# A two-layer graph kernel on one Trainium2 core: a third staging buffer for transposed halves, and their order by row tiles

## The chip, the cores and the metric

The kernel runs on 1 core of one Trainium2 chip. The metric is device time in microseconds, as the median of several runs. A profile is one execution with the hardware profiler; its times are used for single instructions.

## The reference

x is 2048 x 512, adj is 2048 x 2048, both fp32. The constants scale and quantise; what is computed is

```python
h = maximum(layernorm(x), 0)
# layer 0: quantised inputs (15 levels) times quantised weights (7 levels)
support = relu(matmul(quant(h), quant_w(weight)) * scales)
x = x + matmul(adj / s, quant(support)) * s * delta
# layer 1: y = C2 @ Dinv (adj_sym + I) Dinv @ h2, with C2 = adj, adj_sym = (adj + adj.T) / 2
h = maximum(layernorm(x), 0)
deg = sum(adj_sym + eye, axis=1)
x = x + (adj @ (deg**-.5 * (adj_sym + eye) * deg**-.5)) @ h
```

## The kernel before

Both products with adj need it transposed on the partitions. The tile `at` holds adj transposed for all 16 row tiles of 128 rows, each entry as two fp16 halves: hi is the rounded value (times 256) and lo is the rest. adj comes in by 32 units; unit u is one half (1024 columns) of row tile u // 2, 128 x 1024 fp32, 512 KB. There are two ways from a unit to `at`:

- A unit is turned: TensorE transposes it by eight 128 x 128 fp32 transposes into PSUM (`turn`, L1041), ScalarE writes the hi half (`hi_turned`, L487), VectorE adds up the columns (`column_sum`, L702) and writes the lo half (`lo_turned`, L715). ScalarE adds up the rows (`row_sum`, L467).
- A unit is moved: ScalarE writes the hi half untransposed to a stage (`hi_rows`, L476, with the row sums), VectorE the lo half (`lo_rows`, L720), and SyncE issues a DMA transpose for each half from the stage to `at` (`move`, L323). There are two stages, used in turn, in the space of row tile 14 of `at`; a stage is free again when both transposes of the unit that used it have landed (`wait_moved`). Unit 29 has a place of its own in tile 15. Moved are the odd units 3 to 29, and 14, 18, 22 (`EVEN`). For an even moved unit VectorE adds up the columns from `at` (`column_sum_late`, L708). GpSimd adds the odd units 1 to 29 to one tile `acc` (L441, L444), which is turned once, as "acc", and reduced by L848.

Until they are needed for `at`, the places of later row tiles hold loads (`in_tile`), so that a transposed unit of tile 6 or later may be written only when the units waiting in its tile are used up (`waited_in`, `free_slot`).

The stage that the change touches is layer 0. Product r is the 32 matmuls of row tile r (`layer0`, L1062), from r = 0 to 15 in order. Product r waits for its two transposed units, and from 2 to 13 also for `x1_ready` of tile r - 2, whose PSUM bank it uses again. For r = 1 to 13 every engine has a list: `TURNS[r]` and `MOVES[r]` give the units. TensorE turns the first unit of `TURNS[r]` ahead of product r and others inside it. ScalarE and VectorE go through the same r in the order of their programs. VectorE's is shown at L903: first the turned unit, then x1 of tile r - 1 (`x1_tile`, L840 with the statistics L842 and L843), then `lo_rows` of the moves, then late column sums, then pieces of the next stage (`sum_unit`, L886 to L891, and `sum_lo`, L896). GpSimd's addition of a unit waits for `prod_done` of the r in which the unit is moved. SyncE's list (L355) is one queue in order: moves, and the loads of units 20 to 31 (`rows_again`), each of which needs the buffer of an earlier unit; a wait in it holds up everything behind it.

After product 15 come two sweeps (L1126) and the last product (L1163, L1179), which the change doesn't touch.

## Time and profile before

| | us |
|---|---|
| median of 3 runs | 501.84 |
| lowest, highest | 499.54, 502.91 |
| the profiled execution's own time | 499.41 |
| its span | 497.5 |
| TensorE busy | 482.9 |
| VectorE busy | 275.2 |
| ScalarE busy | 136.0 |
| GpSimd busy | 46.5 |

The granted TensorE clock is full in all slices of the page. The product of tile 0 ends at about 45 us, that of tile 15 at 162 us, the sweeps at 329 us. Times in rows count from the start of the span. An instruction's time runs from its start to its end; for TensorE, where instructions overlap, a difference of two starts is the better measure of the pace.

### The profile page before, as it was taken

The numbers are of one execution on the slowest core, as the hardware profiler recorded it, in microseconds if no ns is written. First come the engines' busy times: TensorE is split into PE (matmuls) and PEld (weight loads), VectorE is DVE, ScalarE is ACT, GpSimd is POOL, SyncE is SP. The second block draws the span as 40 slices with busy tenths as digits, with TensorE's granted clock in tenths as the row PEclk, the third lists the DMA queues.
The fourth block names the chain that finished last, engine by engine and source line by source line (L and its number), as shares of the span: only waits on it lengthen the run. The fifth ranks groups of instructions, "written<-read, shape, count | busy, mean of one in ns | idle before, by whom it ended". The sixth has DMA issues, their size and how long they took to land.

```text
span 497.5 us, 6362 instructions
## 1 busy us (share of the span) xinstructions
PE 482.9 (97%) x2390; PEld 236.6 (48%) x2390; DVE 275.2 (55%) x367; ACT 136.0 (27%) x192; POOL 46.5 (9%) x54
## 2 busy tenths in 40 slices
PE   3999998999999999999999999999999999999997
PEld 2755554445554444444444444444444444444446
DVE  6964969989999688785996777340000000000000
ACT  1796634433432343534512122140000000000000
POOL 2322932332200000000000000000000000000000
PEclk9999999999999999999999999999999999999999
DMA  8978996779677233233223231045010000100001
GB/s 296 402 315 191 303 243 130 130 172 208 152 216 288 65 106 124 87 107 104 86 89 122 88 123 42 1 134 224 22 42 21 21 21 21 42 21 21 22 21 43
DMA packets 54731, 60.56 MB, mean 122 GB/s; under 512 B 37688, under 2 KB 37944, under 8 KB 54712
## 3 DMA queue, kind: packets, MB, share of 16 engines
q1 hardware_dynamic: 54704, 60.30, 40.5%
q8 instruction: 12, 0.20, 0.2%
q14 instruction: 7, 0.06, 0.0%
q10 hardware_dynamic: 8, 0.00, 0.0%
HBM read 42.99 MB, written 8.39 MB: 103 GB/s over the span
## 4 chain that ended last, share of the span: by engine, by line
PE 84%; DVE 7%; DMA 3%; SPq 2%; ACT 1%; issue 1%; POOL 0%; ACTq 0%; DVEq 0%; POOLq 0%
PE ps_a L1163 31%; PE ps_p L1062 13%; PE ps_p L1126 7%; PE ps_a L1126 7%; PE ps_b L1126 7%; PE ps_m L1126 4%; PE ps_h L1126 4%; DMA feat<-in_x 2%; DVE at L720 2%; PE ps_b L1013 1%; PE ps_m L1062 1%; PE ps_h L1062 1%; DVE at L715 1%; DVE small L900 1%; PE ps_b L1179 1%
## 5 line engine op out<-in xcount | busy, mean ns | idle before, releaser
L1062 PE MATMUL ps_p<-small,at 128*128 128x512 f16 x448 | 100.0, 379 | 2.0 <-DVE feat L840 2.0
L982 DVE SCALAR_TENSOR_TENSOR feat<-ps_a,feat 128x512 f32<-128x512 f32 (+1 forms) x16 | 10.8, 676 | 148.7 <-PE ps_a L1163 144.2
L1163 PE MATMUL ps_a<-small,at 128*128 128x512 f16 x360 | 80.2, 379 | 0.0
L1163 PE MATMUL ps_a<-a_in,at 128*128 128x512 f16 x360 | 80.2, 379 | 0.0
L1062 PEld LDWEIGHTS ps_p<-small,at 128*128 128x128 f16 x448 | 43.6, 98 | 51.5 <-DVE feat L840 2.5
L551 ACT ACTIVATE split<-a_in 128x1024 f16<-128x1024 f32 x30 | 31.7, 1057 | 101.5 <-PE ps_p L1126 90.0
L1163 PEld LDWEIGHTS ps_a<-a_in,at 128*128 (+1 forms) x360 | 35.2, 98 | 42.5
L1163 PEld LDWEIGHTS ps_a<-small,at 128*128 (+1 forms) x360 | 35.2, 98 | 42.5
L896 DVE TENSOR_TENSOR split<-a_in,split 128x1024 f16<-128x1024 f32 x30 | 36.7, 1224 | 33.7 <-ACT split L551 33.7
L1126 PE MATMUL ps_p<-feat,split 128*128 (+1 forms) x180 | 43.9, 379 | 0.5 <-DVE small L900 0.5
L1126 PE MATMUL ps_a<-feat,split 128*128 (+1 forms) x180 | 43.8, 379 | 0.0
L1126 PE MATMUL ps_b<-feat,split 128*128 (+1 forms) x180 | 43.7, 379 | 0.0
L887 DVE TENSOR_TENSOR a_in<-a_in,at 128x1024 f32<-128x1024 f32 x30 | 36.8, 1226 | 1.0
L886 DVE SCALAR_TENSOR_TENSOR a_in<-a_in,at 128x1024 f32<-128x1024 f32 x30 | 36.5, 1218 | 0.0
L1126 PEld LDWEIGHTS ps_p<-feat,split 128*128 128x128 f16 x180 | 17.5, 98 | 22.0 <-DVE small L900 1.0
L1126 PEld LDWEIGHTS ps_a<-feat,split 128*128 128x128 f16 x180 | 17.6, 98 | 21.4 <-issue 0.5
L1126 PEld LDWEIGHTS ps_b<-feat,split 128*128 128x128 f16 x180 | 17.6, 98 | 21.2
L1126 PE MATMUL ps_m<-feat,split 128*128 (+1 forms) x90 | 24.3, 379 | 0.0
L1126 PE MATMUL ps_h<-feat,split 128*128 (+1 forms) x90 | 24.3, 379 | 0.0
L444 POOL TENSOR_TENSOR at<-at 128x1024 f32<-128x1024 f32 x8 | 21.2, 2648 | 18.4 <-PE ps_p L1062 17.8
L444 POOL TENSOR_TENSOR at<-at,a_in 128x1024 f32<-128x1024 f32 x6 | 15.2, 2537 | 25.4 <-PE ps_p L1062 19.2
L720 DVE SCALAR_TENSOR_TENSOR at<-at 128x1024 f16<-128x1024 f32 x10 | 14.2, 1428 | 4.7 <-ACT at L476 4.7
(179 smaller groups left out, 432.5 us busy)
## 6 DMA issues: line engine op xcount, KB each, us to landing
a_in<-in_adj SPq DMA_DIRECT2D x46, 512.0 KB, 3.9
at<-in_adj SPq DMA_DIRECT2D x16, 512.0 KB, 10.0
out<-feat SPq DMA_DIRECT2D x31, 256.0 KB, 4.2
feat<-in_x SPq DMA_DIRECT2D x8, 512.0 KB, 10.8
feat<-out SPq DMA_DIRECT2D x4, 1024.0 KB, 9.3
at<-in_L_gnn_weight SPq DMA_DIRECT2D x2, 512.0 KB, 3.8
at<-at SPq DMA_TRANSPOSE x34, 3.3
split<-in_adj SPq DMA_DIRECT2D x1, 512.0 KB, 16.2
```

Source lines behind the costliest of these rows:

```text
L444: nc.gpsimd.tensor_tensor(acc, acc, unit_in(u), ALU.add).then_inc(acc_done, 1)
L551: nc.scalar.activation(part(v % 2, 0), sum_in(v), ACT.Copy).then_inc(shi, 1)
L715: nc.vector.scalar_tensor_tensor(at_half(u // 2, 1, u % 2), turn_bank(u)[:, :], SA, at_half(u // 2, 0, u % 2), ALU.mult, ALU.subtract).the ...
L720: nc.vector.scalar_tensor_tensor(stage(u, 1), unit_in(u), SA, stage(u, 0), ALU.mult, ALU.subtract)\
L886: link(nc.vector.scalar_tensor_tensor(u3, u3, SA, at_across(h, 0, j), ALU.mult, ALU.add))
L887: last = nc.vector.tensor_tensor(u3, u3, at_across(h, 1, j), ALU.add)
L896: nc.vector.tensor_tensor(part(v % 2, 1), sum_in(v), part(v % 2, 0), ALU.subtract).then_inc(slo, 1)
L900: nc.vector.scalar_tensor_tensor(z_part(t, 1), BANK[t % B], cz[:, t:t + 1], z_part(t, 0), ALU.mult, ALU.subtract).then_inc(z_ready, 1)
L982: nc.vector.scalar_tensor_tensor(out, products, 1.0 / (SA * SZ), out, ALU.mult, ALU.add).then_inc(y_out, 1)
L1062: last = nc.tensor.matmul(l0_bank(r), at_block(r, lo, j), small[:, j * D:(j + 1) * D], start=(j == 0 and lo == 0), stop=(j == T - 1 and lo ...
L1126: last = nc.tensor.matmul(BANK[t], part(k, lo)[:, t * P:(t + 1) * P], g_part(j, g_lo), start=(first and lo + g_lo == 0), stop=False)
L1163: last = nc.tensor.matmul(BANK[n], at_block(t, lo, j), z_part(j, z_lo), start=(j == 0 and lo + z_lo == 0), stop=(j == T - 1 and lo == 1))
```

## The change

- Unit 10 is moved, too (`EVEN`). Its late column sum is made in r = 5.
- There are three stages: two in tile 14 as before, one in the second half of tile 15. The last three moved units (25, 27, 29) have one each.
- Moves are done a row tile earlier: unit 7 ahead of r = 1, then `MOVES` as written out. Loads are placed by a list `LOADS`; unit 24's load stands behind the move of unit 25.
- VectorE does x1 first in each r.
- GpSimd's additions wait for the product numbers in `ADD_AT`; its first waits for three lo halves instead of two.
- The columns of `acc` are summed by TensorE: eight fp32 matmuls with one column of `mean_of` (1/128) in place of eight transposes, and VectorE scales eight columns in place of reducing 1024.
- Units 14, 15 and 16, 17 exchange their waiting places; row sums of units 1 and 2 are made later.

```diff
--- before.py
+++ after.py
@@ -24,7 +24,7 @@
 GROUPS = (0, 2, 4, 8, 12, T)
 LATE_GROUPS = (0, 13, T)
 LATE_SUMS = (0, 2)
-EVEN = (14, 18, 22)
+EVEN = (10, 14, 18, 22)
 MOVED = tuple(sorted(tuple(range(3, 30, 2)) + EVEN))
 ADDED = tuple(range(1, 30, 2))
 TURNED = tuple(u for u in range(UNITS) if u not in MOVED)
@@ -95,11 +95,14 @@
         w_int = late(13, 2048, KD * D, f16)
         acc = late(15, 0, W, f32)
 
+        def stage_no(u):
+
+            return (MOVED.index(u) - len(MOVED)) % 3
+
         def stage(u, lo):
 
-            if u == 29:
-                return late(15, 2048 + lo * W, W, f16)
-            return late(14, 2048 * (MOVED.index(u) % 2) + lo * W, W, f16)
+            k = stage_no(u)
+            return late(14 + k // 2, 2048 * (k % 2 if k < 2 else 1) + lo * W, W, f16)
         xq = [late(12, 1024 * k, 2 * D, f16) for k in range(2)]
         sq = [late(11, 1024 * k, 2 * D, f16) for k in range(2)]
         hT = [late(10, 1024 * k, 2 * D, f16) for k in range(2)]
@@ -179,7 +182,7 @@
         acc_done = sem("acc_done")
         hi_ready = sem("hi_ready")
         lo_ready = sem("lo_ready")
-        at_moved = [[sem(f"at_moved{k}{lo}") for lo in range(2)] for k in range(2)]
+        at_moved = [[sem(f"at_moved{k}{lo}") for lo in range(2)] for k in range(3)]
         atlo = sem("atlo")
         prod_done = sem("prod_done")
         x1_ready = sem("x1_ready")
@@ -206,11 +209,11 @@
 
         def in_tile(u):
 
-            return (6, 7, 8, 9, 12, 11, 10, 13)[(u - RING) // 2]
+            return (6, 7, 8, 9, 12, 10, 11, 13)[(u - RING) // 2]
 
         def waited_in(u):
 
-            first = 2 * (4, 5, 6, 7, 10, 9, 8, 11)[u // 2 - 6] - 4
+            first = 2 * (2, 3, 4, 5, 7, 8, 6, 9)[u // 2 - 6]
             return first, first + 1
 
         def unit_in(u):
@@ -270,20 +273,22 @@
         TURNS = {r: [2 * r + 4] for r in range(2, 12)}
         TURNS.update({1: [4, 6], 12: [28, "acc"], 13: [30, 31]})
 
-
-        ROW_SUMS = {2: [0, 1], 4: [2, 4], "acc": []}
-
-
-        MOVES = {r: [2 * r + 7] for r in range(2, 12)}
-        MOVES[1] = [7, 9]
         for u in EVEN:
-            MOVES[u // 2 - 4].append(u)
             TURNS[u // 2 - 2] = []
+
+
+        ROW_SUMS = {2: [0], 4: [1, 2, 4], "acc": []}
+
+
+        MOVES = {1: [9, 10], 2: [11, 13], 3: [14, 15], 4: [17], 5: [18, 19], 6: [21], 7: [22, 23], 8: [25],
+                 9: [u for u in (26, 27) if u in MOVED], 10: [29], 11: []}
+        ADD_AT = {u: r + (u < 19) for r in MOVES for u in MOVES[r]}
 
         def wait_moved(engine, u):
             k = MOVED.index(u)
+            same = [w for w in MOVED[:k + 1] if stage_no(w) == stage_no(u)]
             for lo in range(2):
-                engine.wait_ge(at_moved[k % 2][lo], 16 * (k // 2 + 1))
+                engine.wait_ge(at_moved[stage_no(u)][lo], 16 * len(same))
 
 
         def arrivals(u):
@@ -316,12 +321,12 @@
                 for lo, ready in ((0, hi_ready), (1, lo_ready)):
                     sp.wait_ge(ready, MOVED.index(u) + 1)
                     if u == 29:
-                        wait_moved(sp, 25)
-                        wait_moved(sp, 27)
+                        wait_moved(sp, MOVED[-3])
+                        wait_moved(sp, MOVED[-2])
                     elif u >= 12:
                         free_slot(waited_in(u)[lo])
                     sp.dma_start_transpose(at_half(u // 2, lo, u % 2).rearrange("p (b i) -> p b i", i=P), stage(u, lo))\
-                      .then_inc(at_moved[MOVED.index(u) % 2][lo], 16)
+                      .then_inc(at_moved[stage_no(u)][lo], 16)
 
             def store_x1(t):
                 sp.wait_ge(x1_ready, t + 1)
@@ -350,18 +355,22 @@
             move(3)
             move(5)
             sp.wait_ge(sq_ready, T // 2)
-            for u in range(14, 20):
+            rows(14)
+            rows(15)
+            move(7)
+            for u in range(16, 20):
                 rows(u)
+            LOADS = {7: [25], 8: [27, 24, 26], 9: [29], 10: [31, 28], 11: [30]}
             for r in range(1, 12):
-                if r >= 8:
-                    rows_again(2 * r + 9)
+                for u in LOADS.get(r, [])[:1]:
+                    rows_again(u)
                 for u in MOVES[r]:
                     move(u)
-                    if u == 7:
+                    if u == 9:
                         for w in range(AHEAD, AHEAD + 4):
                             rows_again(w)
-                if r >= 8:
-                    rows_again(2 * r + 8)
+                for u in LOADS.get(r, [])[1:]:
+                    rows_again(u)
             for v in range(2, 6):
                 free_slot(UNITS - 6 + v)
                 sums(v)
@@ -434,10 +443,10 @@
 
             for k, u in enumerate(ADDED):
                 pool.wait_ge(arr_sem(u), arrivals(u))
-                if u > 5:
-                    pool.wait_ge(prod_done, next(r for r in MOVES if u in MOVES[r]))
+                if u in ADD_AT:
+                    pool.wait_ge(prod_done, ADD_AT[u])
                 if k == 0:
-                    pool.wait_ge(lo_ready, 2)
+                    pool.wait_ge(lo_ready, 3)
                     nc.gpsimd.tensor_scalar(acc, unit_in(u), 0.0, 1.0, ALU.add, ALU.mult).then_inc(acc_done, 1)
                 else:
                     pool.wait_ge(acc_done, k)
@@ -469,10 +478,10 @@
             def hi_rows(u):
                 k = MOVED.index(u)
                 act.wait_ge(arr_sem(u), arrivals(u))
-                if k < 2:
+                if k < 3:
                     act.wait_ge(w_ready, 2)
                 else:
-                    wait_moved(act, MOVED[k - 2])
+                    wait_moved(act, MOVED[k - 3])
                 nc.scalar.activation(stage(u, 0), unit_in(u), ACT.Copy, scale=SA, accum_out=rowsum[:, u:u + 1])\
                   .then_inc(hi_ready, 1)
 
@@ -489,8 +498,8 @@
 
             def turn_hi(u):
                 if u == 28:
-                    wait_moved(act, 25)
-                    wait_moved(act, 27)
+                    wait_moved(act, MOVED[-3])
+                    wait_moved(act, MOVED[-2])
                 elif u == 30:
                     wait_moved(act, 29)
                 if u != "acc":
@@ -581,6 +590,7 @@
             scale_support(7)
             hi_turned(2)
             hi_rows(5)
+            hi_rows(7)
             for w in ROW_SUMS[2]:
                 row_sum(w)
             for r in range(1, 14):
@@ -830,6 +840,7 @@
             clamp_support(7)
             lo_turned(2)
             lo_rows(5)
+            lo_rows(7)
 
             def x1_tile(r):
 
@@ -845,9 +856,8 @@
             def turned_out(u):
                 if u == "acc":
                     dve.wait_ge(turned, turn_no(u) + 1)
-                    nc.vector.tensor_reduce(colp[:, ADDED[1] * B:(ADDED[1] + 1) * B],
-                                            turn_bank(u)[:, :].rearrange("p (b i) -> p b i", i=P), AXIS.X, ALU.add)\
-                      .then_inc(atlo, 1)
+                    nc.vector.tensor_scalar(colp[:, ADDED[1] * B:(ADDED[1] + 1) * B], turn_bank(u)[:, 0:B], float(P),
+                                            None, ALU.mult).then_inc(atlo, 1)
                 else:
                     column_sum(u)
                     lo_turned(u)
@@ -902,9 +912,9 @@
 
             for r in range(1, 14):
                 now = TURNS[r]
+                x1_tile(r - 1)
                 for u in now[:1]:
                     turned_out(u)
-                x1_tile(r - 1)
                 moves = MOVES.get(r, [])
                 for u in moves[:1]:
                     lo_rows(u)
@@ -915,7 +925,7 @@
                 if r - 4 in LATE_SUMS:
                     column_sum_late(r - 4)
                 for k, u in enumerate(EVEN):
-                    if r == (7, 9, 12)[k]:
+                    if r == (5, 7, 9, 12)[k]:
                         wait_moved(dve, u)
                         column_sum_late(u)
                 if r == 8:
@@ -1036,10 +1046,13 @@
                     pe.wait_ge(atlo, turn_before(u))
                 if turn_no(u) in (2, 3):
                     pe.wait_ge(sup_out, T // 2 - 3 + turn_no(u))
-                source = acc if u == "acc" else unit_in(u)
                 for k in range(B):
-                    last = nc.tensor.transpose(turn_bank(u)[:, k * P:(k + 1) * P], source[:, k * P:(k + 1) * P],
-                                               ident32[:, :])
+                    if u == "acc":
+                        last = nc.tensor.matmul(turn_bank(u)[:, k:k + 1], acc[:, k * P:(k + 1) * P], mean_of[:, 0:1],
+                                                start=True, stop=True)
+                    else:
+                        last = nc.tensor.transpose(turn_bank(u)[:, k * P:(k + 1) * P], unit_in(u)[:, k * P:(k + 1) * P],
+                                                   ident32[:, :])
                 last.then_inc(turned, 1)
 
             def layer0(r, js):
```

## Rows read from the trace of the kernel before

**Rows 1.** The page's part 1, first line: engines, busy us, share, instructions.

```profile
PE 482.9 (97%) x2390; PEld 236.6 (48%) x2390; DVE 275.2 (55%) x367; ACT 136.0 (27%) x192; POOL 46.5 (9%) x54
```

**Rows 2.** Windows: length, busy us (count) by engine, granted clock, DMA share, GB/s.

```profile
46.00:70.00 24.00, 24.00 (x128) 12.81 (x127) 19.41 (x21) 12.17 (x20) 17.28 (x8) 1.00 1.05 279
80.00:148.00 68.00, 68.00 (x349) 34.76 (x347) 64.96 (x66) 26.19 (x41) 15.89 (x6) 1.00 0.73 165
```

**Rows 3.** Timeline of TensorE, products 3 to 5: start, us, engine, line, count, idle before.

```profile
62.36 7.07 PE L1062 MATMUL ps_p<-small,at 128*128 128x512 f16 x32
69.27 1.04 PE L1041 MATMUL ps_b<-ident,at 128*128 128x128 f32 x8
70.14 7.07 PE L1062 MATMUL ps_p<-small,at 128*128 128x512 f16 x32
79.19 7.08 PE L1062 MATMUL ps_p<-small,at 128*128 128x512 f16 x32 [1.97 <-DVE feat L840]
```

**Rows 4.** The chain that ended last, 70 to 79 us: start, us, what.

```profile
70.51 3.19 DMA at<-at
...
74.98 0.98 DVE at L720
...
76.12 1.22 DVE colp L702
77.34 1.13 DVE at L715
78.47 0.67 DVE feat L840
```

**Rows 5.** Timeline of SyncE's queue, each issue by itself.

```profile
59.02 1.97 SPq L298 DMA_DIRECT2D a_in<-in_adj  x4
...
62.75 6.36 SPq L323 DMA_TRANSPOSE at<-at  x1
69.15 1.31 SPq L323 DMA_TRANSPOSE at<-at  x1
70.51 1.34 SPq L323 DMA_TRANSPOSE at<-at  x1
```

**Rows 6.** Groups of VectorE, 80 to 148 us: count, busy us, mean ns.

```profile
L708 DVE TENSOR_REDUCE colp<-at 128x8 f32<-128x2048 f16 x5 | 11.4, 2279 | 0.0
...
L840 DVE SCALAR_TENSOR_TENSOR feat<-ps_p,cst,feat 128x512 f32<-128x512 f32 x9 | 6.7, 742 | 0.0
L842 DVE BATCH_NORM_STATS2 st<-feat 128x6 f32<-128x512 f32 x9 | 6.2, 694 | 0.3
...
L720 DVE SCALAR_TENSOR_TENSOR at<-at 128x1024 f16<-128x1024 f32 x4 | 4.7, 1200 | 0.0
...
L843 DVE BATCH_NORM_AGGREGATE mv<-st 128x2 f32<-128x6 f32 x10 | 1.8, 182 | 0.3
```

**Rows 7.** Timeline near 53 us: an addition of GpSimd and a lo half.

```profile
52.48 2.37 POOL L444 TENSOR_TENSOR at<-at 128x1024 f32<-128x1024 f32 x1 [0.17 <-POOL at L444]
...
53.44 2.49 DVE L720 SCALAR_TENSOR_TENSOR at<-at 128x1024 f16<-128x1024 f32 x1
```

**Rows 8.** Timeline of TensorE, fp32 matmuls at the start; PEld is the weight load.

```profile
8.51 0.50 PEld L997 LDWEIGHTS ps_m<-wstat,mean_of 128*128 128x128 f32 x2 [2.39 <-DVE wstat L743]
...
15.67 3.56 PE L1003 MATMUL ps_b<-mean_of 128*128 128x128 f32 x28
```

**Rows 9.** Timeline: a lo half, then loads, then turns that wait for loads.

```profile
106.80 1.19 DVE L720 SCALAR_TENSOR_TENSOR at<-a_in,at 128x1024 f16<-128x1024 f32 x1
...
109.34 1.01 SPq L298 DMA_DIRECT2D a_in<-in_adj  x2
...
115.48 1.04 PE L1041 MATMUL ps_a<-ident,a_in 128*128 128x128 f32 x8
...
135.29 0.52 SPq L298 DMA_DIRECT2D a_in<-in_adj  x1
...
139.66 0.86 PEld L1041 LDWEIGHTS ps_a<-ident,a_in 128*128 128x128 f32 x8 [0.28 <-DMA a_in<-in_adj]
```

## The prediction

> **What bounds the kernel now.** I read the engine totals first: TensorE is busy for 482.9 of 497.5 us [rows 1]. So nothing that only frees another engine can move the end; the change can gain TensorE work taken out, and TensorE waits taken out. In the stage that is edited TensorE waits once, 1.97 us in front of the product of row tile 5: the product of tile 4 starts at 70.14, runs 6.91 us (62.36 to 69.27 is one such product), and the next starts at 79.19 instead of 77.05 [rows 3]. The wait's own row says 1.97, the starts say 2.14; I use 2.14.
>
> Then the windows: from 46 to 70 the DMA share is 1.05 at 279 GB/s, and from 80 to 148 VectorE is busy for 64.96 of 68 us beside a TensorE that never waits [rows 2]. So the front of this stage is bound by DMA, and its rest has two engines near their limit. That second fact decides much below: VectorE has 3 us to spare in 68.
>
> The chain of waits tells whose wait the 1.97 us is. SyncE's second transpose of unit 11 is issued at 70.51 and lands 3.19 us later, at 73.70; ScalarE can then reuse the stage for unit 14; VectorE makes its lo half at 74.98, turns out unit 12 (76.12, 77.34), and only then does x1 of tile 3 (78.47), for which the product of tile 5 waits [rows 4]. The transposes are late for a reason of their own: the second one of unit 9 sat 6.36 us in SyncE's queue, until 69.11, behind four loads of 512 KB issued at 59.02; the two of unit 11 follow at 69.15 and 70.51, 1.36 us apart [rows 5].
>
> **The change, part by part.**
>
> Unit 10 moved instead of turned. TensorE loses eight transposes: 69.27 to 70.14, 0.87 us [rows 3]. VectorE loses a column sum and a lo half from PSUM (1.22 + 1.13) [rows 4] and gains a lo half of a move and a late column sum (1.20 + 2.28) [rows 6]: 1.1 us more. ScalarE loses the row sum. DMA and SyncE gain two transposes at 1.36 us: 2.7 us, put in front of unit 11.
>
> The sum of acc by eight matmuls of one column. VectorE's reduction, of the size of the column sum's 1.22 us [rows 4], becomes one of eight columns, and lies on no path that TensorE waits for. For TensorE no row has this form in a running stream. From below: eight blocks at the pace of the eight transposes, 0.87 us, so nothing added. From above: the fp32 matmuls of L1003 give two records each, 28 records in 3.56 us, the last one 0.28 long, so 0.122 us apart; 16 records are 1.95 us, 1.08 more than now. L997 has one column, and still its two weight loads end 0.50 us after they start, so the load, not the column count, sets the pace [rows 8]. I take 16 loads at 0.109 (0.87/8, one load's pace in the transposes), 1.74 us: +0.87. It lies between two parts of product 12 with nothing beside it.
>
> The Trainium skill, TensorE: Matmul & The Clock Gate, section Back-to-back issue gap, gives an issue floor of about 25 ns for matmuls of 1 to 64 columns; by it 16 records would be an estimated 0.4 us and the term -0.5, while the same page's section LDWEIGHTS, about 107 ns for 128 columns, gives 1.7 us and +0.8. The L997 row sides with the second.
>
> Third stage, and moves one tile earlier. A stage is free when the unit three back has landed, not two. That helps only where a stage, and not DMA, is what is late. Up to 69.11 the queue is full in the kernel before, and all its loads and transposes (units 5, 7, 9, six and four loads) still stand in front of unit 11 after the change, now with two transposes of unit 10 as well. So I let unit 11 land at 73.70 + 2 x 1.36 = 76.4. Unit 15, three back, is now in the same row tile as unit 14, and VectorE's program puts both lo halves in front of x1 of tile 3. From landing to lo half is 1.28 us (73.70 to 74.98), the lo half 1.14, and x1 to TensorE 0.72 (78.47 to 79.19) [rows 3, 4]: 76.4 + 3.1 = 79.6. Product 5 could start at 77.05 - 0.87 = 76.2, so the wait does not go but grows from 2.1 to 3.4; against before the product starts 79.6 - 79.19 = +0.4 late. Bounds: unit 11 lands as before at 73.7, then product 5 starts at 76.9, -2.3; or GpSimd's addition of unit 17, released by product 4 at 76.2, catches the lo half, +0.9 on top, as L720 took 2.49 us at 53.44 when an addition ran from 52.48 to 54.85, and 1.20 otherwise [rows 6, 7].
>
> x1 first in each tile. It costs nothing, as unit 12 would not be turned before; it gains the 2.35 us of the turned unit, 76.12 to 78.47 [rows 4]. That gain is inside the 79.6 above: the second lo half and the later landing use it up. It helps all later tiles, where x1 would be the first thing TensorE waits for.
>
> Loads. The load of unit 24 waited for the lo half of unit 23; it now stands behind the transposes of unit 25, so behind the lo half of 25. This is new and I price it. After x1 of tile 3 (80.4 with its statistics) VectorE turns out unit 12 (82.7); up to the lo half of unit 25 it then has seven lo halves of 1.13, four late column sums of 2.2, four x1 tiles of 1.6 and two turned units of 2.3, 27.7 us in all [rows 4, 6]: 110.4, and I add 0.65, half of one meeting with GpSimd (2.49 - 1.20) [rows 6, 7]: 111.0. In the kernel before, the lo half of unit 23 starts at 106.80 and ends at 107.99; the load goes out at 109.34, 1.35 later, and a load issued at 135.29 let TensorE go at 139.66, 4.37 later [rows 9]. So unit 24 is there at 116.8. TensorE wants it after five products and two turns from 79.6, at 115.9. A new wait of 0.9. Bounds: none, if VectorE is ahead; and 3 if it meets GpSimd at three more lo halves.
>
> GpSimd's sums spread. Additions come one product earlier from unit 19 on. They are not on the path. They use what VectorE's operations with two SBUF inputs use, and come right after a product, where VectorE now does x1 and then either a turned unit (PSUM, no meeting) or a lo half (a meeting). Taken at the 0.65 above.
>
> After product 15 nothing is touched. The sum: +0.4 (product 5 later; in it -2.1 old wait, -0.9 unit 10, +3.4 new wait) + 0.9 (unit 24) + 0.87 (acc) = +2.2. The profiled execution's span of 497.5 becomes 499.7. Its own time was 499.41, and the median of the runs shown 501.84 is 2.4 above that; on the median: 504.0.
>
> **The rivals.**
>
> Transposes land in time (faster). The DMA share of 1.05 counts waiting packets, and 279 GB/s is not a high rate; if the new order is served better, unit 11 lands at 73.7 though two more stand before it. Product 5 then starts 2.3 us earlier than now, VectorE is 2.7 us further, and unit 24 causes about 0.5 or nothing: -2.3 + 0.87 + 0 to 0.5 = -1.2, time 500.6. Against it: SyncE's 6.36 us [rows 5]. If also acc costs nothing, 499.4. Chance 0.25.
>
> The order changes nothing that counts: the waits stay as they are, unit 10 gives 0.87 and acc takes 0.87. Time 501.8. For it: VectorE's work stays nearly the same. Chance 0.12.
>
> VectorE becomes the bound (slower). One mechanism: six additions after product 4 each catch a lo half, 1.3 each, 7.8 in all. VectorE has 3.0 us to spare, and my schedule leaves x1 little room: unit 12 turned out at 82.7, a lo half 1.1, a late column sum 2.2 and x1 of tile 4 itself 0.7 make 86.8, and product 6 wants it at 79.6 + 6.9 + 0.9 = 87.4 [rows 3, 4, 6]. From 3 us of meetings on, every further one delays TensorE: 7.8 - 3.0 = 4.8, less the 0.65 counted, +2.2: +6.3, time 508.2. Against it: three of the six are followed by a turned unit. Chance 0.13. The forecast has the rest, 0.50.
>
> **How the numbers follow.** Predicted 504.0. Half of the forecast's case lies within 502.5 to 505.5. Leaving out a tenth on either side, 499.4 (the faster rival with its cheap acc) to 507.5, most of the way to the slower one. Within 1% is 496.8 to 506.9, about what a measurement can tell from no change. Faster by over 1% needs 5 us, more than all TensorE waits and unit 10 in this stage (3.0): 0.02. Slower by over 1% is the slower rival: 0.12. The rest 0.86.
>
> **What the profile would show.** Right: a TensorE wait of about 3.4 us in front of product 5, ended by x1 of tile 3, near 79.6; a wait near 116 in front of a turn, ended by DMA; the acc matmuls taking 1.7 us; VectorE nearly without idle time from 80 to 148. Wrong: product 5 starting at 76 to 77; the loads of units 24 and 26 out before 110; L1041 in the acc turn under 1 us. What would make it wrong first is the landing of unit 11, on which the first two terms both hang.

## The result and the profile after

The changed kernel takes 506.38 us (six runs, 504.88 to 507.87), the kernel before 500.79 us in the same comparison: ratio 1.0109, 95% interval 1.0080 to 1.0138. It is 5.6 us slower. The profiled execution has a span of 505.5 us, 8.0 more than the 497.5 of before. The prediction's range of 499.4 to 507.5 holds it; the forecast of 504.0 was 2.4 us too low, and the forecast change of +2.2 us was 3.4 us too low.

The page of the changed kernel, the line that answers to [rows 1], and the granted clock in 40 slices:

```profile
PE 484.8 (96%) x2390; PEld 237.0 (47%) x2390; DVE 278.5 (55%) x367; ACT 135.0 (27%) x191; POOL 47.7 (9%) x54
...
PEclk9999998999999999999999999999999999999999
```

TensorE has 1.9 us more busy time with the same number of instructions (8 fewer for unit 10, 8 more for acc), and one slice of the clock is low. The timeline of TensorE in the changed kernel (start, us, line, count, idle before), to be read beside [rows 3]:

```profile
70.13 7.08 PE L1075 MATMUL ps_p<-small,at 128*128 128x512 f16 x32
81.49 8.77 PE L1075 MATMUL ps_p<-small,at 128*128 128x512 f16 x32 [4.28 <-DVE feat L851]
90.09 1.04 PE L1054 MATMUL ps_b<-ident,at 128*128 128x128 f32 x8
...
120.22 1.09 PE L1054 MATMUL ps_b<-ident,a_in 128*128 128x128 f32 x8 [0.59 <-DMA a_in<-in_adj]
...
138.19 1.09 PE L1054 MATMUL ps_b<-ident,a_in 128*128 128x128 f32 x8 [2.19 <-DMA a_in<-in_adj]
139.12 1.89 PE L1075 MATMUL ps_p<-small,at 128*128 128x512 f16 x8
140.84 1.84 PE L1051 MATMUL ps_a<-mean_of,at 128*128 128x1 f32 x16
142.54 5.34 PE L1075 MATMUL ps_p<-small,at 128*128 128x512 f16 x24
```

The wait in front of product 5 has grown from 1.97 to 4.28 us, and product 5 itself takes 8.6 us (81.49 to 90.09) instead of 6.9. The turns of units 24 and 28 wait for loads, and the columns of acc take 1.70 us. The first sweep starts at 170.19; before, at 162.19. The 8.0 us are, up to rounding:

| | us |
|---|---|
| the turn of unit 2 starts at 42.23, not 41.59, ahead of anything that was changed | 0.64 |
| product 5 starts later than before, from there (81.49 to 79.19) | 1.66 |
| product 5 runs longer | 1.69 |
| turn of unit 24: wait, by starts | 0.75 |
| turn of unit 28: wait, by starts | 2.35 |
| acc, 1.70 instead of 0.87 | 0.83 |

The first term is scatter: in the traces shown here the turn of unit 2 starts anywhere from 40.96 to 42.91. So below I give, for each trace, the stage's length from that turn to the first matmul of the sweep: 120.6 us before, 128.0 after. What comes behind the stage is the same in all. One trace is one execution; the ratios are over all runs. The terms without the scatter come to 7.3 us, more than the 5.6 of the medians, as the profiled execution of the changed kernel (507.60) lies 1.2 above its median and that of the kernel before (499.41) 1.4 below; the terms are the sizes of one pair of executions.

### The profile page after: what moved, and what is told of

It reads as the page before. It is cut to its first block, busy times and chain, and to the rows that moved or that the text cites. A ratio compares the mean times of both kernels' runs of the same rounds, so it can differ in the third digit from the quotient of the medians.

```text
span 505.5 us, 6362 instructions
## 1 busy us (share of the span) xinstructions
PE 484.8 (96%) x2390; PEld 237.0 (47%) x2390; DVE 278.5 (55%) x367; ACT 135.0 (27%) x191; POOL 47.7 (9%) x54
## 4 chain that ended last, share of the span: by engine, by line
PE 73%; DVE 14%; DMA 6%; ACT 3%; SPq 2%; issue 1%; POOL 0%; ACTq 0%
PE ps_a L1176 31%; PE ps_p L1139 7%; PE ps_a L1139 7%; PE ps_b L1139 7%; DVE at L730 4%; PE ps_p L1075 4%; PE ps_m L1139 4%; PE ps_h L1139 4%; DMA at<-at 3%; DMA feat<-in_x 2%; DVE colp L718 2%; PE ps_b L1023 1%; PE ps_m L1075 1%; PE ps_h L1075 1%; SPq L328 1%; DVE split L906 1%
## 5 line engine op out<-in xcount | busy, mean ns | idle before, releaser
L1075 PE MATMUL ps_p<-small,at 128*128 128x512 f16 x448 | 101.5, 384 | 4.3 <-DVE feat L851 4.3
L906 DVE TENSOR_TENSOR split<-a_in,split 128x1024 f16<-128x1024 f32 x30 | 36.7, 1224 | 34.0 <-ACT split L560 34.0
L897 DVE TENSOR_TENSOR a_in<-a_in,at 128x1024 f32<-128x1024 f32 x30 | 36.8, 1225 | 1.0
L896 DVE SCALAR_TENSOR_TENSOR a_in<-a_in,at 128x1024 f32<-128x1024 f32 x30 | 36.5, 1218 | 0.0
L730 DVE SCALAR_TENSOR_TENSOR at<-at 128x1024 f16<-128x1024 f32 x11 | 19.1, 1755 | 9.8 <-ACT at L485 9.8
L453 POOL TENSOR_TENSOR at<-at 128x1024 f32<-128x1024 f32 x8 | 22.4, 2797 | 9.0 <-PE ps_p L1075 8.2
```

The lines of the kernel that those rows point to most:

```text
L453: nc.gpsimd.tensor_tensor(acc, acc, unit_in(u), ALU.add).then_inc(acc_done, 1)
L730: nc.vector.scalar_tensor_tensor(stage(u, 1), unit_in(u), SA, stage(u, 0), ALU.mult, ALU.subtract)\
L896: link(nc.vector.scalar_tensor_tensor(u3, u3, SA, at_across(h, 0, j), ALU.mult, ALU.add))
L897: last = nc.vector.tensor_tensor(u3, u3, at_across(h, 1, j), ALU.add)
L906: nc.vector.tensor_tensor(part(v % 2, 1), sum_in(v), part(v % 2, 0), ALU.subtract).then_inc(slo, 1)
L1075: last = nc.tensor.matmul(l0_bank(r), at_block(r, lo, j), small[:, j * D:(j + 1) * D], start=(j == 0 and lo == 0), stop=(j == T - 1 and lo ...
```

## Why product 5 waits, and why it is slow

The changed kernel's timelines of ScalarE, VectorE and GpSimd at that place:

```profile
76.58 1.06 ACT L485 ACTIVATE at<-at 128x1024 f16<-128x1024 f32 x1 [1.46 <-DMA at<-at]
```

```profile
77.76 3.01 DVE L730 SCALAR_TENSOR_TENSOR at<-at 128x1024 f16<-128x1024 f32 x1 [1.38 <-ACT at L485]
80.69 0.74 DVE L851 SCALAR_TENSOR_TENSOR feat<-ps_p,cst,feat 128x512 f32<-128x512 f32 x1
...
89.47 4.49 DVE L730 SCALAR_TENSOR_TENSOR at<-at 128x1024 f16<-128x1024 f32 x2
...
115.99 3.25 DVE L897 TENSOR_TENSOR split<-split,at 128x1024 f32<-128x1024 f32 x1
...
124.40 2.53 DVE L906 TENSOR_TENSOR split<-split 128x1024 f16<-128x1024 f32 x1
```

```profile
77.35 2.34 POOL L453 TENSOR_TENSOR at<-at 128x1024 f32<-128x1024 f32 x1 [5.66 <-PE ps_p L1075]
```

Unit 11 has landed at 76.5, within 0.1 us of the 76.4 predicted (0.6 earlier, if the later start is taken off). ScalarE's hi half of unit 15 waited for it, VectorE's lo half follows at 77.76, and meets GpSimd's addition of unit 17, which product 4 had released at 77.35. The addition ends at 79.69; the lo half at 80.77, 1.08 later, as if it had started when GpSimd was done. Then comes x1 of tile 3. The same is seen at 89.47, 99.92 (1.69 us instead of 1.20), 115.99 and 124.40. The Trainium skill, GPSIMD Engine Reference, section Specifications, says that the two engines share SBUF interfaces and contend where a VectorE instruction has two SBUF inputs; the trace agrees: L730, L897 and L906, with two such inputs, get 1.8, 2.0 and 1.3 us longer.

The kernel before has such meetings too, but none between 77 and 109 us. Its two longest in this stage after that are of L887, which takes 1.23 us undisturbed:

```profile
109.16 3.26 DVE L887 TENSOR_TENSOR split<-split,at 128x1024 f32<-128x1024 f32 x1
...
125.36 3.27 DVE L887 TENSOR_TENSOR tmp<-tmp,at 128x1024 f32<-128x1024 f32 x1
```

With L896 at 117.57 (1.64 instead of 1.22 us) they add up to 4.5 us. In the changed kernel they add up to 7.8 us, and 4.4 of these come before 102 us, where the kernel before has none. So what the change adds is 3.3 us, and, more than that, their place: in or ahead of the lo halves that x1 of tile 3 and the load of unit 24 wait for.

The windows of the changed kernel around the wait (length, busy us of PE, PEld, DVE, ACT, POOL, granted clock, DMA share, GB/s):

```profile
77.00:81.50 4.50, 0.23 (x2) 0.02 (x2) 3.71 (x3) 3.69 (x7) 3.98 (x2) 1.00 0.97 186
81.50:84.00 2.50, 2.50 (x7) 0.96 (x8) 2.47 (x4) 1.28 (x4) 1.49 (x1) 0.57 1.05 197
84.00:87.00 3.00, 3.00 (x12) 1.24 (x11) 3.00 (x3) 1.15 (x2) 0.00 (x0) 0.79 0.47 92
87.00:90.00 3.00, 3.00 (x16) 1.40 (x14) 2.93 (x5) 0.00 (x0) 0.00 (x0) 1.00 0.90 173
```

After 4.3 us of idle TensorE the granted clock was 0.57 for 2.5 us and 0.79 for 3 (of its two levels, 1.2 and 2.4 GHz, mostly the lower one at first). That is the 1.69 us.

## The experiments

Of each kernel, the ratio to the kernel before is given, beside 1.0109 for the changed kernel; 0.001 is 0.5 us.

**a_x1early**: x1 of tile 3 ahead of the lo half of unit 15.

```diff
-                x1_tile(r - 1)
+                if r != 4:
+                    x1_tile(r - 1)
...
                 for u in moves[:1]:
                     lo_rows(u)
+                if r == 3:
+                    x1_tile(3)
```

> The changed kernel, with VectorE's x1 of tile 3 put ahead of the lo half of unit 15 (it waited behind it, while the product before had ended at 77.0). Theory 1 (the wait of 4.28 us in front of product 5 is that order, and the fall of the granted clock after it comes from that idle time): product 5 starts near 78 with a wait under 1 us, runs 6.9 us instead of 8.6, clock 1.00. Yet the turns of units 24 and 28 wait for loads that VectorE's lo halves of 25 and 29 let go, so TensorE gives most of it back there: VectorE comes 1 to 2 us forward, the end 1 to 2.5 us. Rival (the 4.28 us and the slow product add up undiminished to the end): 4 to 5.5 us faster than the changed kernel. Third (the transposes alone are late): product 5 still waits over 3 us.

Ratio 1.0055 (1.0035 to 1.0076), so 2.7 us faster than the changed kernel; the stage is 123.3 us long, 4.6 less. TensorE's timeline:

```profile
76.51 7.08 PE L1078 MATMUL ps_p<-small,at 128*128 128x512 f16 x32 [0.27 <-DVE feat L851]
83.42 1.04 PE L1057 MATMUL ps_b<-ident,at 128*128 128x128 f32 x8
86.12 13.99 PE L1078 MATMUL ps_p<-small,at 128*128 128x512 f16 x64 [1.66 <-DVE feat L851]
...
115.36 1.09 PE L1057 MATMUL ps_b<-ident,a_in 128*128 128x128 f32 x8 [0.57 <-DMA a_in<-in_adj]
...
132.44 1.09 PE L1057 MATMUL ps_b<-ident,a_in 128*128 128x128 f32 x8 [1.30 <-DMA a_in<-in_adj]
```

Product 5 waits 0.27 us and runs 6.91 at full clock. But product 6 now waits 1.66 for x1 of tile 4, and both turns still wait for their loads. So the order was the cause of the 4.28 us, and part of the gain is given back, as theory 1 has it. In front of and in product 5, 5.7 us are gone (4.28 to 0.27, and 8.60 to 6.91); by the ratio about half of them reach the end. The expected 1 to 2.5 us was a little low.

**a_loads**: the loads of units 24 and 28 in front of the moves of 25 and 29.

```diff
-            LOADS = {7: [25], 8: [27, 24, 26], 9: [29], 10: [31, 28], 11: [30]}
+            LOADS = {7: [25], 8: [24, 27, 26], 9: [29], 10: [28, 31], 11: [30]}
```

> The changed kernel, with the load of unit 24 ahead of that of 27 and of the transposes' sequel as far as the queue allows: in r = 8 unit 24 is loaded in front of the moves of 25, and in r = 10 unit 28 in front of those of 29. Theory 1 (the waits of 0.59 and 2.19 us in front of these two turns are the order of the queue): both vanish, and the end comes about 3 us forward. Rival (VectorE's lag takes the time back, as x1 of tiles 8 to 10 is then what TensorE waits for): 0 to 1.5 us. Product 5 keeps its wait of 4.3 us and its 8.6 us in both.

Ratio 1.0114 (1.0051 to 1.0177); the interval is too wide to tell 3 us from none (three of the four runs are at 504.4 to 504.8 us, one at 509.3). In the trace both waits are gone, as theory 1 has it, and the stage is 126.0 us long, 1.9 less and not 3. The difference is the clock again (TensorE's timeline and a window):

```profile
80.59 10.04 PE L1075 MATMUL ps_p<-small,at 128*128 128x512 f16 x32 [4.28 <-DVE feat L851]
```

```profile
80.60:85.60 5.00, 5.00 (x12) 1.78 (x13) 4.97 (x6) 2.37 (x5) 1.49 (x1) 0.50 0.79 150
```

The same wait of 4.28 us cost 3.0 us in this execution (9.89 instead of 6.91), as the clock stood at 0.50 for 5 us. The price of an idle time of this size changes from one execution to the next.

**a_warm**: the idle time in front of product 5 filled.

```diff
             def layer0(r, js):
+                if r == 5 and js[0] == 0:
+                    for _ in range(16):
+                        nc.tensor.matmul(ps_h[:, 0:P], mean_of[:, :], mean_of[:, :], start=True, stop=True)
```

> The changed kernel, with 16 spare matmuls (fp32, 128x128, into a PSUM bank that nobody reads) between product 4 and the wait of product 5; they take about 3.9 of the 4.28 idle us. Theory 1 (the clock fell because TensorE stood idle): the granted clock stays at 1.00 through product 5, which runs 6.9 us instead of 8.6. The end moves by 0 to 0.5 us only, since the two loads are what the later turns wait for. Rival A (the clock falls at this place for another reason): product 5 still 8.6 us. Rival B (what product 5 loses goes to the end undiminished): the end 1.7 us forward.

```profile
77.74 3.73 PE L1061 MATMUL ps_h<-mean_of 128*128 128x128 f32 x32
81.31 7.07 PE L1078 MATMUL ps_p<-small,at 128*128 128x512 f16 x32
...
119.60 1.09 PE L1054 MATMUL ps_b<-ident,a_in 128*128 128x128 f32 x8 [1.83 <-DMA a_in<-in_adj]
```

The clock stayed at 1.00 and product 5 took 6.91 us: the idle time was the cause of the slow product. The runs agree: the mean granted clock was 0.993 to 0.997 in all six runs of the changed kernel, and 1.00 in three of the four runs here. The wait for unit 24 grew from 0.59 to 1.83 us. Ratio 1.0100 (1.0061 to 1.0140), 0.5 us faster than the changed kernel, which is not clear of noise: theory 1. In this trace the wait for unit 28 was 1.38, and the stage 125.9 us, 2.1 less than in the changed kernel's trace, of which the runs show 0.5.

**a_x1loads**: both edits, of a_x1early and a_loads.

> The edits of a_x1early and a_loads together. Theory 1 (two causes that hide each other: whichever is taken away alone, the other holds TensorE back): together more than the sum of the two alone, 5 to 6.5 us faster than the changed kernel, near the kernel before. Rival (VectorE is the bound from 80 us on, with 3 us to spare): 3 to 4.5 us.

Ratio 1.0056 (1.0027 to 1.0085), no better than a_x1early alone. The stage in the trace is 122.3 us, 5.6 less than in the changed kernel, in the span of theory 1; but this trace is of the fastest of the ten runs (501.26 us), and the others don't show it. In place of the loads there is a new wait, for VectorE's lo half of a turned unit, in front of the sums of acc:

```profile
134.43 1.92 PE L1054 MATMUL ps_a<-mean_of,at 128*128 128x1 f32 x16 [1.15 <-DVE at L725]
```

By the ratios it is 2.7 us, below the rival's 3 to 4.5 and further still from theory 1. In this trace what remains is VectorE. In four of the ten runs the mean granted clock was 1.00 (501.3 to 501.7 us) and in six below it (502.5 to 506.2 us), so a wait that lowers the clock seems to come back in some runs; no trace shows where.

**a_noadd**: GpSimd's additions of units 17 to 29 cut to 8 of 1024 columns (that part of the column sums is left out).

```diff
-                    nc.gpsimd.tensor_tensor(acc, acc, unit_in(u), ALU.add).then_inc(acc_done, 1)
+                    n = W if u < 17 else 8
+                    nc.gpsimd.tensor_tensor(acc[:, 0:n], acc[:, 0:n], unit_in(u)[:, 0:n], ALU.add).then_inc(acc_done, 1)
```

> The changed kernel, with GpSimd's additions of units 17 to 29 cut from 1024 to 8 columns (a part of the column sums is left out; order and semaphores stay). Theory 1 (the meetings of these additions with VectorE's operations with two SBUF inputs put VectorE back by about 7.7 us between 77 and 127, as the long L730, L897 and L906 in the changed kernel's trace add up): VectorE's operations all take their short time, product 5 starts 1.8 us earlier, the waits for the loads of units 24 and 28 go, 4 to 6.5 us faster than the changed kernel. Rival (VectorE's lag doesn't reach TensorE): 0 to 1.8 us.

Ratio 1.0024 (1.0006 to 1.0043), 4.3 us faster than the changed kernel; the stage is 122.6 us, 5.3 less. Theory 1. VectorE's lo half of unit 15 takes its short time, the loads are there in time, and TensorE's wait in front of product 5 is 2.26 us:

```profile
78.12 1.22 DVE L731 SCALAR_TENSOR_TENSOR at<-at 128x1024 f16<-128x1024 f32 x1 [1.47 <-ACT at L486]
```

```profile
80.06 8.65 PE L1076 MATMUL ps_p<-small,at 128*128 128x512 f16 x32 [2.26 <-DVE feat L852]
```

What is left of the loss, with no meeting at all after unit 15, is this wait, the clock after it (8.5 us for the product) and acc. It also shows that 2.26 us of idle time can lower the clock, while 1.97 us in the kernel before [rows 3] and 2.62 us in the trace of a_u10 (next) did not. Nor did it do so in each run: in six of the ten the mean granted clock was 1.00 (500.2 to 501.4 us), and the trace is of one of the others (502.84).

The edit takes away all 7.8 us of meetings and not only the 3.3 that the change adds. No run cuts the additions in the kernel before alone; by its trace nothing is to be won there, as TensorE waits for nothing between product 5 and 139 us.

**a_u10**: unit 10 turned again, all else as changed.

```diff
-EVEN = (10, 14, 18, 22)
+EVEN = (14, 18, 22)
...
-        MOVES = {1: [9, 10], 2: [11, 13], ...
+        MOVES = {1: [9], 2: [11, 13], ...
...
-                    if r == (5, 7, 9, 12)[k]:
+                    if r == (7, 9, 12)[k]:
```

> The changed kernel, with unit 10 turned again (its two transposes gone from in front of unit 11's, its turn back in TensorE's program, its late column sum gone); everything else as in the changed kernel. Theory 1 (these two transposes make unit 11 land 2.7 us later, and so the lo half of unit 15 and x1 of tile 3): x1 of tile 3 is ready before product 4 ends, product 5 starts without a wait of note, its clock stays at 1.00, and VectorE is 3 to 5 us ahead: 4 to 5 us faster than the changed kernel. Rival (unit 10 costs DMA nothing that counts): 0.9 us slower, the turn alone, and product 5 still waits over 3 us.

Ratio 1.0018 (1.0000 to 1.0036): 4.5 us faster than the changed kernel, theory 1. TensorE's timeline:

```profile
69.96 13.98 PE L1075 MATMUL ps_p<-small,at 128*128 128x512 f16 x64
...
115.94 1.09 PE L1054 MATMUL ps_a<-ident,a_in 128*128 128x128 f32 x8 [2.62 <-DMA a_in<-in_adj]
```

Products 4 and 5 are one group of 64: no wait, though x1 still stood behind the lo half of unit 15. Unit 11 landed at 73.3 us instead of 76.5, and this lo half ran from 74.55 to 75.8, ahead of the addition, which started at 77.17. So two transposes of unit 10 in front of those of unit 11, 2.7 us of DMA, decided product 5, and the meeting with it. The wait for unit 24 is still there, with 2.62 us; the clock stayed at 1.00 behind it, and the product after the turn took 6.90 us.

**b_third**: the third stage alone, in the kernel before.

```diff
+        def stage_no(u):
+
+            return (MOVED.index(u) - len(MOVED)) % 3
...
-                if k < 2:
+                if k < 3:
                     act.wait_ge(w_ready, 2)
                 else:
-                    wait_moved(act, MOVED[k - 2])
+                    wait_moved(act, MOVED[k - 3])
```

> The kernel before, with the third stage alone (order of moves, loads and VectorE's program as before; unit 10 turned). Theory 1 (a stage that frees with unit 9 and not with unit 11 lets the lo half of unit 14 come 2.5 us earlier, at 72.4, as unit 9 has landed at 71.2): the wait of 2.14 us in front of product 5 goes, 2 us faster. Rival (DMA is what is late, whatever the stages): wait and time unchanged.

The trace is theory 1's: VectorE's lo half of unit 14 at 72.27 instead of 74.98 [rows 4], x1 of tile 3 at 75.84, no wait, and a stage of 118.5 us, 2.1 less than before.

```profile
72.27 1.38 DVE L724 SCALAR_TENSOR_TENSOR at<-at 128x1024 f16<-128x1024 f32 x1 [1.92 <-ACT at L480]
...
75.84 0.73 DVE L844 SCALAR_TENSOR_TENSOR feat<-ps_p,cst,feat 128x512 f32<-128x512 f32 x1
```

Median 497.85 against 499.37 us, but the ratio is 0.9990 (0.9956 to 1.0023): seven of ten runs lie at 496.3 to 498.4 and three at 502.1 to 502.5. So over all runs the gain is not clear of noise, and no trace shows what the three have.

**b_x1first**: x1 first alone, in the kernel before.

```diff
+                x1_tile(r - 1)
                 for u in now[:1]:
                     turned_out(u)
-                x1_tile(r - 1)
```

> The kernel before, with x1 first in each of VectorE's row tiles, nothing else. Theory 1 (product 5 waits because x1 of tile 3 stands behind the turned unit 12): x1 at 76.2 instead of 78.5, the wait of 2.14 us goes, 2 us faster. Rival (VectorE's turned units come later by 1.6 us each, and TensorE, which needs them for a product or a bank, waits there): 0 to 1 us slower.

Ratio 1.0071 (1.0049 to 1.0092): 3.5 us slower. Neither expectation held. The wait of product 5 did go (TensorE's first wait in this stage is at 116), but the turn of unit 24 waits 3.25 us, with the clock lower after it (0.67 from 116 to 119). VectorE, GpSimd, SyncE's queue and TensorE:

```profile
83.88 4.32 DVE L720 SCALAR_TENSOR_TENSOR at<-at 128x1024 f16<-128x1024 f32 x2
```

```profile
83.62 2.36 POOL L444 TENSOR_TENSOR at<-at 128x1024 f32<-128x1024 f32 x1 [4.54 <-PE ps_p L1062]
```

```profile
111.40 1.01 SPq L298 DMA_DIRECT2D a_in<-in_adj  x2
```

```profile
116.12 1.16 PE L1041 MATMUL ps_a<-ident,a_in 128*128 128x128 f32 x8 [3.25 <-DMA a_in<-in_adj]
117.07 8.74 PE L1062 MATMUL ps_p<-small,at 128*128 128x512 f16 x32
```

GpSimd's addition starts at the end of a product. In the kernel before, up to 101 us, VectorE then works on a turned unit in PSUM, on x1 or on a late column sum, or has its lo half already under way. With x1 first, the lo halves come right behind, and the pair at 83.88 takes 4.32 us instead of the 2.33 that a pair takes undisturbed; the single one at 91.96 takes 2.87 and the pair at 98.55 takes 4.33. The load of unit 24 goes out at 111.40 instead of 109.34 [rows 9]. SyncE's queue waits for VectorE's lo halves there and nowhere for GpSimd.

**b_x1noadd**: the same, with the additions cut as in a_noadd (that part of the column sums is left out).

> b_x1first (x1 first in the kernel before, which waited 3.25 us for the load of unit 24) with the same additions cut to 8 columns (a part of the column sums left out). Theory 1 (x1 first puts the lo halves right behind the end of a product, where GpSimd's addition starts too, and these meetings let the load of unit 24 out late): that wait goes, and 4 us or more faster than b_x1first, 2 us faster than the kernel before. Rival (the order itself delays the load): the wait stays above 2 us.

Ratio 0.9938 (0.9921 to 0.9955): 6.6 us faster than b_x1first and 3.1 faster than the kernel before. TensorE waits nowhere in the stage (118.4 us); unit 24 is turned at 113.15, and its load goes out at 106.30. VectorE's pairs take 2.33 and 2.42 us again. The pair b_x1first and b_x1noadd shows that it is the meetings that made x1 first slower.

**b_thirdx1**: third stage and x1 first.

> The kernel before with both, the third stage and x1 first. Theory 1: they take away one and the same wait, so 2 us faster than the kernel before and not 4, and less scatter, since no idle time is left that lets the granted clock fall. Rival (each takes away something of its own): 3 us or more.

Median 497.38 us, ratio 0.9981 (0.9946 to 1.0016). Six of ten runs are at 496.5 to 497.5, one at 498.0 and three at 502.2 to 503.0; its trace is of the run at 502.21 and has the 3.38 us wait for unit 24. So the median is theory 1's, though the interval holds 1, and "less scatter" was wrong.

**b_acccol**: acc's columns by matmuls, in the kernel before.

> The kernel before, with the columns of acc summed by eight fp32 matmuls of one column instead of eight transposes and a reduction. Theory 1 (the weight load sets the pace): these take 1.7 us instead of 0.87 and the end comes 0.8 us later. Rival (VectorE's 1.1 us saved count): 0 to 0.3 us faster.

Ratio 1.0013 (1.0000 to 1.0026), 0.7 us slower; by the starts in the trace 0.84:

```profile
133.99 1.84 PE L1040 MATMUL ps_b<-mean_of,at 128*128 128x1 f32 x16
135.70 5.34 PE L1064 MATMUL ps_p<-small,at 128*128 128x512 f16 x24
```

```profile
133.78 1.97 PEld L1040 LDWEIGHTS ps_b<-mean_of,at 128*128 128x128 f32 x16
```

Sixteen records in 1.71 us, 0.107 apart with one column each, while the weight loads (PEld) run without a gap: the weight load sets the pace. Theory 1.

**b_thirdloads**: b_third, and from r = 8 on both loads in front of the moves.

```diff
                 if r >= 8:
                     rows_again(2 * r + 9)
+                    rows_again(2 * r + 8)
                 for u in MOVES[r]:
...
-                if r >= 8:
-                    rows_again(2 * r + 8)
```

> b_third (third stage in the kernel before) with both loads of r = 8 to 11 in front of the moves of that r, so that unit 24's doesn't wait for the lo half of unit 23. Theory 1 (the 3 of 10 runs of b_third near 502 us are runs in which VectorE met GpSimd and that load came late): all runs near 497.5 us, 2 us faster than the kernel before. Rival (these runs have another cause): they stay, about 3 in 10.

Ratio 0.9966 (0.9947 to 0.9984), 498.24 us against 499.61: 1.7 us faster than the kernel before, and 7 faster than the changed one. It beats both, and is the only kernel with the whole computation whose interval lies below 1. Its five runs are all between 497.58 and 498.64. If runs near 502 us still came three times in ten, five without one would be seen in one case of six; so that the order of the loads took them away is likely and not shown. The order of the loads without the third stage was not run.

## Why the prediction was right or wrong, point by point

**The number.** 506.38 us lies in the range, but that 504.0 came so near is in part luck. I had added +2.2 to 501.84, the median of three runs, and the median of six is 500.79, 1.05 lower; the change itself is +5.6, two and a half times what I forecast. The terms of the sum that I had were right in kind; two were missing, the clock and unit 28, which make 4.0 us in the trace, and a third, the meeting at unit 15, stood only in a bound.

**Product 5, forecast +0.4 us, measured +1.7.** The step on the landing of unit 11 was right (76.4 against 76.5), and so was what follows from it: the wait grows in place of going. a_u10 and a_x1early show both halves, the two transposes and the order of VectorE's program. Wrong was the value taken between the bounds: I left out the meeting of the lo half with the addition of unit 17, though by my own numbers product 4 ended at 76.2 and the lo half started at 77.7, inside an addition of 2.4 us. The bound "+0.9 on top" was the likely case. It gives +1.3, and the 0.9 doesn't follow from the rows beside it, which give 2.49 - 1.20 = 1.29 and with it +1.7, as measured. The meeting itself cost 1.8.

**The clock, no term, measured +1.7.** The kernel before has an idle time of 1.97 us and full clock after it, and I priced a longer wait as only its length. a_warm shows that the idle time causes the fall. This step was missing, and the trace of a_noadd shows that 2.26 us of idle time are enough for it in some runs.

**Unit 24, forecast +0.9, measured 0.75.** Right by place and mechanism: the order of SyncE's queue behind VectorE's lo half (a_loads). The size is luck. It is the difference of two times, and both came 3 to 4 us late: the lo half of unit 25 ended at 114.8 and not at 111.0, as VectorE had met GpSimd three times and not half a time, and TensorE was ready for the turn at 119.6 and not at 115.9, as product 5 was late and slow.

**Unit 28, no term, measured 2.35.** The same edit moves the load of unit 28 behind the moves of 29, and I followed it only for 24. The load of unit 28 was in the same list of the diff, and it stands behind a lo half just as the other does.

**acc, forecast +0.87, measured 0.83** (0.84 in b_acccol). The weight load sets the pace, as the L997 row had it; of the Trainium skill's two sections on TensorE: Matmul & The Clock Gate, LDWEIGHTS gives the measured time and the issue floor does not.

**Unit 10, a gain of 0.87 for TensorE**, is real and was more than paid for: a_u10, without it, is 4.5 us faster.

**The slower rival** named the mechanism that tells most of the loss after product 5: VectorE put back by meetings. They add up to 1.8 + 2.2 + 0.5 + 2.0 + 1.3 = 7.8 us in the trace. That the rival had 7.8, too, is chance: five operations and not six, one of them L897 and one L906 and no lo halves, and 4.5 us of meetings stand in the kernel before already, inside the 64.96 us of [rows 2] to which the rival added its own. Its price of +6.3 is near the 5.6 measured, but of these the clock, which it had not, is a part. I gave it 0.13; on a VectorE with 3 us to spare in 68, and additions released at just the moment where x1 first puts the lo halves, it deserved as much as the forecast. a_noadd, 4.3 us faster, shows its weight; but the waits for the two loads go as well with a_loads, which leaves the meetings in, so they need both the meetings and the new order of the loads.

**x1 first "costs nothing"** was wrong: b_x1first is 3.5 us slower, and the pair with b_x1noadd shows why. **The third stage** I judged useless, as DMA and not a stage was late. For the changed order no run takes it out, so that isn't shown. In the old order the trace of b_third shows that it takes the wait away, since unit 14's stage was free and its lo half started 2.7 us earlier (72.27 and 74.98); over all runs this gain is not clear of noise.

**Not tested by themselves** are the moves one tile earlier, the new places of units 14 to 17, and the new product numbers for GpSimd's additions. The terms of the table leave less than 0.1 us of the trace's difference for them, beyond their part in the waits that it lists.

## What to carry to other kernels

Where the work of one engine makes another's longer, as the additions did here, an order of work has to be read for both: the start of one engine's work is tied to the end of a product, and a harmless exchange in the other's program can put its sensitive operations right there. A transfer put in front of a queue that is full delays all behind it by its own length (here two transposes, 2.7 us), so what it saves has to be weighed against the next one that somebody waits for. And when one load in a queue is found to be late, look at every other load that the same edit moved.

## What the runs showed of the hardware

The granted clock of TensorE fell after idle times of 4.28 us (0.57, then 0.79; in another execution 0.50 for 5 us), of 2.26 us in a_noadd and of 3.25 us in b_x1first, but not after 1.97 us in the kernel before, 2.19 us in the changed kernel (at 138), 2.62 us in a_u10, nor after the 3.38 us in the trace of b_thirdx1, whose product then took 6.9 us. So the length of the idle time alone doesn't tell. A product after such a wait took 6.9, 8.5, 8.6 or 9.9 us. An idle time thus has a price beyond its length that one execution doesn't give.

An operation of VectorE with two SBUF inputs, begun during an addition of GpSimd, ended 1.1 us after the addition (79.69 and 80.77; 1.07 to 1.09 in the other meetings named here), whatever it had been given before: nearly its whole time of 1.2 us comes after. A meeting thus costs what was left of the addition, up to about 2 us, not the 1.3 us that I took from [rows 7].
